# A vision tower kernel on one core: scores before collections, routing steps on three engines, injects and states in pairs, and expert weights applied by VectorE from PSUM

## The reference

```python
def reference(x, ...):
    h = tok(x)                       # 8x8 windows, 8 heads, 2-D rotary q and k, softmax(q k) v, projection
    h = h + mamba(layernorm(h))      # rmsnorm, in_proj, 4-tap conv, silu, then the scan below, gate, out_proj
    h = h + experts(layernorm(h))    # 6 experts of 3 layers, the best 2 of a token weighed and added
...
        def step(h, inp):
            dA_t, xdb_t, c_t = inp
            h = dA_t * h + xdb_t
            y_t = jnp.einsum('bdn,bn->bd', h, c_t)
            return (h, y_t)
...
        rh = jax.nn.relu(features @ router_w1 + router_b1)
        expert_logits = jax.nn.softmax(rh @ router_w2 + router_b2, axis=-1)
        top_w, top_i = jax.lax.top_k(expert_logits, TOP_K)
        routing_weights = jax.nn.softmax(top_w, axis=-1)
...
        sel = jnp.take_along_axis(expert_out, top_i[:, :, :, None], axis=2)
        combined = jnp.sum(sel * routing_weights[..., None], axis=2)
```

## Time and profile before

| | us |
|---|---|
| median of 3 runs (1891.58 to 1894.5) | 1894.16 |
| the profiled execution, its own time | 1909.17 |
| its span, first to last instruction | 1907.4 |
| first scan of chunk 0 | 191.3 |
| last scan of chunk 15 | 1832.1 |
| a steady round, mean of nine (604.28 to 1574.87) | 107.84 |
| the round read closely here (928.65 to 1035.57) | 106.92 |

### The profile page before, as it was taken

How to read it: one execution, slowest core, us unless ns; L and a number is a source line. 1 busy time by engine, 2 the same in 40 slices (tenths; PEclk the granted TensorE clock), 3 DMA queues, 4 the chain that set the end, 5 groups by cost and what they waited for, 6 DMA issues and landing times. The chain is left out here.

```text
span 1907.4 us, 27554 instructions
## 1 busy us (share of the span) xinstructions
PE 1406.5 (74%) x8708; PEld 642.9 (34%) x8708; DVE 1355.3 (71%) x1835; ACT 1036.6 (54%) x1909; POOL 1210.2 (63%) x1667
## 2 busy tenths in 40 slices
PE   3775768786969778686968778686968778676565
PEld 1552424151524324152524324252523424121211
DVE  1112787868688787868788777878787787978941
ACT  2224646565655646565655646565565656565432
POOL 2113586767676675766777675767776676877651
PEclk9857978797968879696878878697877778687765
DMA  2003685666667575766756575676756476777820
GB/s 64 3 12 89 164 248 143 200 177 168 189 163 188 135 208 152 192 179 164 195 155 188 138 207 163 174 188 174 190 155 184 137 207 168 198 201 213 220 72 6
DMA packets 215209, 303.86 MB, mean 159 GB/s; under 512 B 79436, under 2 KB 79640, under 8 KB 214936
## 3 DMA queue, kind: packets, MB, share of 16 engines
q1 hardware_dynamic: 215064, 302.10, 57.5%
HBM read 274.75 MB, written 20.97 MB: 155 GB/s over the span
## 5 line engine op out<-in xcount | busy, mean ns | idle before, releaser
L1285 POOL TENSOR_TENSOR hc<-hs,c_rep 128x512 f32<-128x512 f32 x512 | 651.8, 1273 | 380.8 <-DVE hs L1035 380.5
L1035 DVE TENSOR_TENSOR_SCAN hs<-bank,state,xd 128x512 f32<-128x512 f32 x512 | 651.5, 1276 | 56.9 <-issue 49.5
L787 ACT ACTIVATE bank<-dl,a_neg 128x512 f32<-128x512 f32 x512 | 351.5, 688 | 377.3 <-DVE hs L1035 371.1
L1026 DVE TENSOR_TENSOR xd<-xd,bank 128x512 f32<-128x512 f32 x512 | 337.4, 664 | 62.8 <-PE bank L433 62.8
L553 PE MATMUL bank<-q_diag,k_heads 128*128 128x128 f32 x1024 | 199.6, 320 | 6.5 <-ACT top_row L780 5.0
L553 PEld LDWEIGHTS bank<-q_diag,k_heads 128*128 128x128 f32 x1024 | 171.7, 207 | 62.3 <-issue 52.3
L448 PE MATMUL bank<-hc,wts 128*32 128x512 f32 x1024 | 182.6, 774 | 4.6 <-POOL hc L1285 4.1
L714 PE MATMUL bank<-e,wts 64*64 64x512 f32 x384 | 85.6, 975 | 125.9 <-ACT e L967 125.9
L1055 DVE TENSOR_REDUCE neg_max<-bank 128x8 f32<-128x512 f32 x128 | 87.0, 688 | 106.9 <-PE bank L541 106.2
L438 PE MATMUL bank<-top_sel,zeros 128*128 128x512 bf16 x496 | 154.1, 427 | 0.0
L541 PE MATMUL bank<-k_heads,q_diag 64*64 64x512 f32 x512 | 91.2, 789 | 79.5 <-DVE neg_max L1055 47.4
(11 more groups left out here) (175 smaller groups left out, 2500.6 us busy)
## 6 DMA issues: line engine op xcount, KB each, us to landing
xd<-xdel_rows SPq DMA_DIRECT2D x512, 256.0 KB, 4.1
dl<-delta_rows SPq DMA_DIRECT2D x512, 256.0 KB, 3.8
delta_rows<-delta SPq DMA_DIRECT2D x16, 512.0 KB, 6.8
xdel_rows<-xdel SPq DMA_DIRECT2D x16, 512.0 KB, 3.7
xin<-in_x_dram SPq DMA_DIRECT2D x32, 128.0 KB, 2.5
q_diag<-rot SPq DMA_DIRECT2D x64, 64.0 KB
out_dram<-res SPq DMA_DIRECT2D x256, 16.0 KB
k_heads<-rot SPq DMA_DIRECT2D x128, 16.0 KB
```

Source lines behind the costliest of these rows:

```text
L787: act.activation(decay_ps[n % 2][:, :], dl[:, n % 4, :], ACT.Exp, scale=a_neg[:, g:g + 1])\
L1026: dve.tensor_tensor(xd[:, n % 8, :], xd[:, n % 8, :], b_ps[:, :], ALU.mult).then_inc(injected.sem, 1)
L1035: dve.tensor_tensor_scan(hs[:, n % 4, :], decay_ps[n % 2][:, :], xd[:, n % 8, :], state[:, g:g + 1], ALU.mult, ALU.add).then_inc(scanned.s ...
L1285: pool.tensor_tensor(hc[:, n % 8, :], hs[:, n % 4, :], c_rep[:, BAND * h:BAND * h + BAND], ALU.mult)\
```

## The change

- **Attention.** `AT` moves maxima, transposed scores and values one slot earlier. The scores keep their slots but stand first in a slot on PE, ahead of collections and routing. On DVE the maxima stand behind the scan and the feed. The transposition of maxima is a slot earlier. POOL adds the queries in slot 14 instead of 13, and SP issues their copies in slot 15 instead of 14.
- **B.** `spread_b` is at slots 13 and 29.
- **Pairs.** `feed` multiplies two slots' `xd` in one instruction of 128x1024, at even slots and at 15 and 31; POOL writes the states of two scans in one instruction at odd slots. Scan n, for even n, so waits until POOL has finished with scan n-3.
- **Routing.** 13 instructions stay on DVE (slots 15, 17, 18, 20, 21), 10 go to POOL (15 to 21), 4 are on ACT (16 and 19, two of them new: a Relu with a very large scale makes the mask). The factor of the softmax is divided out later, so one product falls away.
- **Weighing.** DVE multiplies `ew` by the weight row directly from the PSUM bank, slots 24 to 29. ACT's copies and POOL's products are gone. The third layers are at slots 26, 28, 30.
- **Moved.** `keep` of 3 columns goes from DVE to ACT. The first layer norm goes from slots 12 to 21 to slots 20 to 29. The eight steps of x times delta on POOL are at slots 12 and 15 to 21 instead of 12 to 19, and SP stores the two results at slots 20 and 22 instead of 18 and 20.
- **Fillers.** 32 in a round instead of 31, at other slots: two are new at slot 6.

```diff
-AT = {"S": [9, 11, 13, 15], "max": [10 + _w for _w in range(NW)],
-      "T": [19, 20, 22, 23, 25, 26, 28, 29], "P": [21, 21, 24, 24, 27, 27, 30, 30]}
-FILLERS = {7: 4, 8: 5, 11: 5, 16: 1, 23: 6, 24: 1, 25: 1, 26: 5, 27: 2, 30: 1}
+AT = {"S": [9, 11, 13, 15], "max": [9 + _w for _w in range(NW)],
+      "T": [18, 19, 21, 22, 24, 25, 27, 28], "P": [20, 20, 23, 23, 26, 26, 29, 29]}
+FILLERS = {6: 2, 7: 4, 8: 5, 11: 5, 16: 1, 23: 6, 24: 1, 25: 3, 26: 3, 29: 2}
+SOFT = (12, 15, 16, 17, 18, 19, 20, 21)
...
-                        if n == 14:
+                        if n == 15:
                             queries(c + 3)
...
-                if s == 18:
+                if s in AT["S"]:
+                    scores(k, 2 * AT["S"].index(s))
+                if s == 17:
                     use = A["top"]
...
-                for e, slot in enumerate((27, 29, 31)):
+                for e, slot in enumerate((26, 28, 30)):
...
-                pe.wait_ge(weighed.sem, weighed.at(k, 2 * e + 2))
+                pe.wait_ge(W[f"wb_{EP + e}"].drained, W[f"wb_{EP + e}"].empty(k))
...
-                    if has(c) and n == 14:
+                    if has(c) and n == 13:
                         spread_b(c, odd, 1)
-                    if has(c + 1) and n == 30:
+                    if has(c + 1) and n == 29:
                         spread_b(c + 1, 1 - odd, 0)
...
-                if 24 <= n < 24 + 2 * EP:
-                    i = n - 24
-                    use = W[f"wb_{PAIRED[i]}"]
-                    act.wait_ge(use.filled, use.full(k))
-                    if i > 1 or past(k - 1):
-                        act.wait_ge(weighed.sem, weighed.at(k, i - 1))
-                    copy(wb[:, i % 2, :], use.bank[:, :]).then_inc(use.drained, 1)
...
+                pair = xd[:, n % 8:n % 8 + 2, :]
+                dve.tensor_tensor(pair, pair, b_ps[:, :].unsqueeze(1).to_broadcast([128, 2, BAND]), ALU.mult)\
+                   .then_inc(injected.sem, 1)
...
-                    dve.wait_ge(stated.sem, stated.at(k, n - 3))
+                    dve.wait_ge(stated.sem, stated.at(k, (n - 4) // 2 + 1))
...
+                if 24 <= n < 24 + 2 * EP:
+                    j = PAIRED[n - 24]
+                    use, made = W[f"wb_{j}"], G[f"h2_{j - EP}"] if j >= EP else F[f"h2_{j}"]
+                    dve.wait_ge(made.drained, made.empty(k))
+                    dve.wait_ge(use.filled, use.full(k))
+                    dve.tensor_tensor(ew[:, j, :], ew[:, j, :], use.bank[:, :], ALU.mult).then_inc(use.drained, 1)
...
-                if 25 <= n < 25 + 2 * EP:
-                    i = n - 25
-                    j = PAIRED[i]
-                    pool.wait_ge(W[f"wb_{j}"].drained, W[f"wb_{j}"].empty(k))
-                    pool.tensor_tensor(ew[:, j, :], ew[:, j, :], wb[:, i % 2, :], ALU.mult).then_inc(weighed.sem, 1)
```

More of the change, by code:

```diff
@@ L851, in prepare @@
             def prepare(k, q, n):
+                if n == 1:
+                    if past(k - 1):
+                        act.wait_ge(Bk["z1"].filled, Bk["z1"].full(k - 1))
+                        act.wait_ge(Bk["n1"].drained, Bk["n1"].empty(k - 1))
+                    act.activation(xnT[:, 0:3], xnT[:, CH:CH + 3], ACT.Copy, scale=col("keep", k, k + 1))\
+                       .then_inc(tail_kept.sem, 1)
                 for s, i2 in ((2, 0), (3, 1)):
@@ L1158, in route @@
                     dve.wait_ge(done.sem, done.at(k, 6))
[L1159 to L1161 removed]
+                    dve.scalar_tensor_tensor(out=st[:, 13, :], in0=st[:, 17, :], scalar=-1.0, in1=st[:, 12, :],
+                                             op0=ALU.add, op1=ALU.mult).then_inc(done.sem, 1)
@@ L1204, in body @@
                     k, s = attention_at(c, n)
+                    if has(c):
+                        scan(c, n)
+                    if n % NU == NU - 1 or (n % 2 == 0 and n % NU != NU - 2):
+                        near = ahead(c, n, 1 + (n + 1) % 2)
+                        if near:
+                            feed(*near)
                     if has(k):
                         maxima(k, s)
-                    if has(c):
-                        scan(c, n)
-                    for i in {0: (), 1: (1, 2)}.get((n + 2) % NU, (2,)):
-                        near = ahead(c, n, i)
-                        if near:
-                            feed(*near)
                     if has(c - 1) and n == 2:
```

199 lines of the change are left out of this document (101 added, 98 removed).

## The result

| | before | after |
|---|---|---|
| median, us | 1892.87 (1891.51 to 1894.5, 4 runs) | 1742.72 (1741.34 to 1745.44, 4 runs) |
| ratio, 95% interval | | 0.921 (0.919 to 0.922) |
| span of the profiled execution | 1907.4 | 1743.6 |
| mean granted clock of TensorE | 0.79 | 0.86 |

A forecast was written before the change was run, and what follows sets the result against it. VectorE's chain of 32 scans and its waits set the round. Terms -8.4, +1.7 and -0.3 gave -7.0 a round, 99.9 us; with the ends -105 us, a median of 1790 us (own bounds 1755 to 1825, stated range 1715 to 1865).

The forecast's parts named there:

- Scan 12 to 23: Stretch of a round with routing and scores: from 45.8 to 37.4 us, -8.4 (-11.6 to -2.8), with first scores held by query copies.
- Scores first: In scan 12 to 23, VectorE's 4.3 us wait a round for scores goes once they stand ahead of L611.
- VectorE's lighter routing: In scan 12 to 23, routing on VectorE falls from 11.1 us a round to 4.5, saving 6.6 (5.5 to 8.5).
- Scan 0 to 12: Stretch of a round with SiLU, 39.6 us: copies `pv` now stand ahead of SiLU; net -0.3 us (-2.5 to +3).
- What ACT itself lost later, the 2.41 us: In scan 0 to 12, ACT's wait for scan 9; delta can come that much earlier, not the reciprocal's whole 7.7 us.
- Scan 23 to 0: Stretch of a round with weighing, 21.6 us: VectorE gains six products, waits go, weight rows come late; 23.3, +1.7 (-1 to +5).
- The rival with this mechanism: Weighing in slots 24 to 31: TensorE pauses for VectorE, falls to 1.2 GHz, up to 15 us more; near 1990 us; chance 0.08.
- More comes back: Rival for all stretches: TensorE stays at 2.4 GHz, copies do not hold scores; 94.5 us a round, 1720 to 1745; chance 0.20.
- POOL in VectorE's place: Rival for slots 15 to 21: VectorE waits for POOL's routing, 3 us a round; 103 a round, or 1835 us; chance 0.16.
- A sign of being wrong: Forecast wrong if VectorE waits most for POOL or ACT, or the last stretch's granted clock is below 0.8.
- Paired feeds: VectorE's feeds by two: save 0.05 us each, need transfers one slot sooner, with 1.4 us left; costed at nothing.
- The two SBUF inputs: VectorE instructions with two SBUF inputs contend with POOL, 1204 against 208 ns; the weighing product from PSUM is not held.

## Why the prediction was right, and where it was not

- **Scan 12 to 23, -8.4 against -7.2.** The floor that the copies set held: first scores were forecast 22.0 us behind scan 12, and L543 starts at 911.32, 21.8 behind 889.54, after waiting for its last copy:

```profile
906.52 2.62 SPq L352 DMA_DIRECT2D q_diag<-rot  x4
...
911.32 1.09 PE L543 MATMUL bank<-k_heads,q_diag 64*64 64x512 f32 x8 [1.07 <-DMA q_diag<-rot]
```

  The stretch came to 38.2 in that round, 37.4 was said. But the two terms on the way were of very unequal worth. Scores first, put at 4.3, measured 3.8 undone. **VectorE's lighter routing, put at 6.6, measured 0.8** (1.3 with the pause shortened): 5.8 us of busy time went, and waits took their place. The stretch's sum did not rest on the 6.6: the prediction saw that the copies would hold the scores, took 37.4 for that and not 34.2, yet still named the routing as the largest saving.
- **Scan 0 to 12, -0.3 against -3.8.** This is the mis-sized term, 3.5 of the 3.7 us a round that came on top. "What ACT itself lost later, the 2.41 us" was too little:

```profile
881.54 1.28 ACT L779 ACT_TABLE_LOAD   x1
882.83 1.30 ACT L789 ACTIVATE bank<-dl,a_neg 128x512 f32<-128x512 f32 x2
```

  Scan 12 is 6.7 us behind the end of the second table load (882.82 to 889.54), where it was 11.5 (956.73 to 968.23): 4.8 came back. What the reciprocal held was not ScalarE's one decay but the projection behind it: the step that reads its result (L1084 before, L1092 after) started 10.9 us behind the table load before (967.62, itself 2.16 us late) and 6.1 after (888.93, 0.43 late), and scan 12 stands right behind that step in both. SiLU's delay was also 1.0 us, not 2.1 (its parts, 1.4 and 0.9, make 2.3; the table load is 24.6 us behind scan 0, where 23.6 and 2.1 make 25.7). 4.8 - 1.0 = 3.8. Undoing the attention's slots gave back 4.1, so they account for all of it, and the clock's part was a few tenths. The weighing is a condition of it, not a further share: the prediction took POOL's six products as a gain of the stretch in which they stand, and the run without that edit shows their backlog in this one, 8 us.
- **Scan 23 to 0, +1.7 against +0.1.** 23.3 was said, though the parts given (20.5, 1.5, 0.2 and 0.8) add up to 23.0; rounds come out at 21.2 or 25.2, neither of which was foreseen. The base was a short round, 21.6 us. The kernel before already had two kinds, five rounds of 21.5 to 21.6 us with 3.4 us at 1.2 GHz and seven of 23.3 to 23.8 with 10.2, 22.7 in the mean, and the prediction missed that. The loop of product and weight row is there, but its price is decided by the clock: 21.2 with TensorE at 2.4 GHz throughout, 25.2 with 10 us of it at 1.2 GHz. The rival with this mechanism had the condition right in kind (a pause for VectorE, then the lower level) and far too dear: up to 15 us against 4. The mean clock of the stretch over twelve rounds, 0.91, stayed above the 0.8 named as a sign of being wrong.
- **More comes back.** This rival's range, 1720 to 1745, holds the time, but not by its mechanism: the scores are held by the copies as the forecast had it, and the clock is 0.78 in that stretch. Only in scan 0 to 12 did TensorE stay at 2.4 GHz, and there it was worth a few tenths. That the range held owes something to luck: this rival's lower end, and not the forecast's own 1755, is what took the time in.
- **POOL in VectorE's place** was put at 3 us a round for two exposed hand-overs. VectorE does wait for POOL, 29.1 us in nine rounds, 3.2 each. The 1.2 us of it that were taken away bought the stretch nothing, as the transfer behind it was waited for instead; the other 2.0 were not tried.
- **A sign of being wrong** did come: VectorE was not to wait for POOL or ScalarE most, and its largest wait is the 56.7 us ahead of scans 8 and 10, for decays of ScalarE. The prediction named the decay of scan 10 as what is late next, but gave its wait no price.
- **Paired feeds**, costed at nothing with 1.4 us left for their transfers: the transfer does come late, 1.82 us in slot 18, and still the pairs with B are worth 2.1 us a round.
- **Ends.** Rounds 13 to 15 gave 21.4 for 18, the tail 5.2 for nothing.
- **The two SBUF inputs** held as said: L1158 takes 1.01 us next to 0.19 for its neighbours, and the product from PSUM 670 ns with POOL at work, where 664 was put.

Not tried: the paired feeds and the slots of B apart, and the layer norm's new slots alone. Why the lower clock follows the pause in slot 24 in one round and not in the next is open; that no round is long with the product first and the pause at 1.7 us is shown.

## What to carry to other kernels

When work is moved off the busiest engine, price the move by what ends last in that stretch after it, and not by the busy time that leaves: 5.8 us of VectorE's time bought 0.8 us of their stretch, and at most 1.4 us of a round (with the pause shortened), while two edits of order alone, scores first and the attention a slot sooner, bought 5.4 and 3.2 us a round. Look for the price of a loaded engine one stretch later than its load, since a backlog shows where it is waited for. And where TensorE waits for a product, make that product first in its slot: two steps of 0.6 us ahead of it cost 10 us here, through rounds in which TensorE ran at 1.2 GHz behind the pause.

## What the runs showed of the hardware that was not expected

- A pause of TensorE of 2.87 us was followed by about 10 us at 1.2 GHz (granted clock 0.54 over 11 us) in four rounds of nine, and eight matmuls of a collection took 1.93 us in them instead of 1.07. A pause of 1.68 at the same place was followed by 3.4 us of it at most. The kernel before, with pauses of 1.38 and 1.31 us there, had 10.2 us of it in seven rounds of twelve.
- A DMA issue occupies ScalarE's queue 0.71 us (four in 2.85), as long as one of its 128x512 instructions (0.69).
